# Depthwise taps of one layer spread over three engines: two of DVE's five made by ACT and added by Pool

## The reference, cut to what matters

```python
def _L2_conv_ref(x, w_dw, w_pw):
    C = x.shape[1]
    u_dw, s_dw = _quant_per_channel_dw(w_dw)
    y = lax.conv_general_dilated(x, _ste(w_dw, u_dw), window_strides=(1, 1), padding=((1, 1), (1, 1)),
                                 dimension_numbers=DN, feature_group_count=C)
    y = y / s_dw
    u_pw, s_pw = _quant_global(w_pw)
    y = lax.conv_general_dilated(y, _ste(w_pw, u_pw), window_strides=(1, 1), padding=((0, 0), (0, 0)),
                                 dimension_numbers=DN)
    return y / s_pw
...
x = x + _L2_conv_ref(_gn(x), L2_conv_w_dw, L2_conv_w_pw)
```

## Time and profile before

| | us |
|---|---|
| median of 3 runs | 474.39 |
| lowest, highest | 474.2, 477.4 |
| the profiled execution | 480.05 |
| its span, first to last instruction | 478.3 |
| PE busy in the span | 399.5 |
| DVE busy | 336.7 |
| ACT busy | 246.6 |
| POOL busy | 195.4 |

### The profile page before, as it was taken

The page is one execution under the profiler, slowest core; times in us unless marked ns, Lnnn a source line. Parts: engine busy times, 40 slices in busy tenths (PEclk is TensorE's granted clock), DMA queues, the critical chain, the costliest instruction groups (busy, mean ns, idle before and its releaser), DMA issues.

```text
span 478.3 us, 14126 instructions
## 1 busy us (share of the span) xinstructions
PE 399.5 (84%) x4971; PEld 290.6 (61%) x4971; DVE 336.7 (70%) x786; ACT 246.6 (52%) x554; POOL 195.4 (41%) x326
## 2 busy tenths in 40 slices
PE   0257889999998978899999999999979895758673
PEld 0257578888887856678787787877753221334341
DVE  0588388777877727767777677777827997576782
ACT  0010567877787354566566655666343321465772
POOL 8011166667566714443434344443531534012212
PEclk9999999999999889999999999999998999576985
DMA  8700000000000000000000000000000000000101
GB/s 283 137 5 0 1 3 3 1 0 0 0 0 0 1 2 1 1 3 1 0 0 0 0 0 0 0 0 0 2 3 0 0 0 1 0 16 17 30 21 49
DMA packets 8510, 7.01 MB, mean 15 GB/s; under 512 B 5058, under 2 KB 8130, under 8 KB 8354
## 3 DMA queue, kind: packets, MB, share of 16 engines
q1 hardware_dynamic: 3984, 5.26, 3.6%
q10 hardware_dynamic: 4498, 1.38, 1.7%
HBM read 5.06 MB, written 1.57 MB: 14 GB/s over the span
## 4 chain that ended last, share of the span: by engine, by line
PE 68%; DVE 13%; issue 7%; ACT 6%; DMA 3%; POOL 1%; DVEq 1%; ACTq 1%; POOLq 0%
PE bank L752 11%; PE bank L779 11%; PE bank L720 11%; PE bank L761 9%; PE bank L730 6%; PE bank L1294 5%; PE bank L822 4%; DVE conv L1213 3%; PE bank L809 3%; DMA table<-in_L_conv_rpb_table 3%; PE bank L1222 2%; PE bank L561 2%; PE bank L824 1%; DVE stats L590 1%; ACT kvT L1329 1%
## 5 line engine op out<-in xcount | busy, mean ns | idle before, releaser
L978 POOL TENSOR_TENSOR probs<-probs,row_max 128x384 f32<-128x384 f32 x128 | 105.2, 828 | 125.5 <-DVE row_max L942 124.4
L938 DVE TENSOR_TENSOR probs<-bank,bias 128x384 f32<-128x384 f32 x128 | 65.4, 553 | 58.3 <-PE bank L752 58.0
L843 ACT ACTIVATE probsT<-bank 128x384 f32<-128x384 f32 x128 | 60.9, 492 | 66.7 <-PE bank L761 66.7
L942 DVE TENSOR_REDUCE row_max<-probs 128x6 f32<-128x384 f32 x128 | 68.2, 545 | 0.9
L761 PE MATMUL bank<-cst,probs 128*128 128x128 f32 x384 | 63.0, 282 | 0.0
L752 PE MATMUL bank<-k,q 64*64 64x128 f32 x1536 | 58.4, 284 | 3.9 <-ACT k L888 2.2
L779 PE MATMUL bank<-v,probsT 128*64 128x18 f32 (+1 forms) x1536 | 57.9, 220 | 1.7 <-ACT probsT L843 0.9
L779 PEld LDWEIGHTS bank<-v,probsT 128*64 128x64 f32 x1536 | 50.3, 138 | 13.3 <-issue 11.2
L752 PEld LDWEIGHTS bank<-k,q 64*64 64x64 f32 x1536 | 42.7, 136 | 24.6 <-issue 24.5
L904 DVE COPY v<-bank 64x384 f32<-64x384 f32 (+1 forms) x96 | 46.7, 487 | 11.9 <-PE bank L730 9.7
L761 PEld LDWEIGHTS bank<-cst,probs 128*128 128x128 f32 x384 | 44.7, 142 | 10.3 <-issue 4.4
(11 more groups left out here) (143 smaller groups left out, 622.3 us busy)
## 6 DMA issues: line engine op xcount, KB each, us to landing
rel_bc<-in_L_conv_rel_index SPq DMA_DIRECT2D x1, 2048.0 KB, 9.3
x<-in_x SPq DMA_DIRECT2D x4, 384.0 KB, 12.3
out_dram<-y_out SPq DMA_DIRECT2D x8, 192.0 KB, 2.1
w<-in_L_conv_w_qkv ACTq DMA_DIRECT2D x1, 432.0 KB, 5.0
cst<-in_consts ACTq DMA_DIRECT2D x1, 421.0 KB
p<-in_L_conv_w_out ACTq DMA_DIRECT2D x1, 144.0 KB, 4.9
pos<-in_L_conv_pos_emb SPq DMA_DIRECT2D x8, 2.0 KB
b_qk<-in_L_conv_qkv_b ACTq DMA_DIRECT2D x8, 0.1 KB, 6.9
```

What stands on the lines that cost most here:

```text
L843: nc.scalar.activation(probsT[w][:, :], ps_probsT[w % 2][:, 0:NP * 128], ACT.Exp).then_inc(L.s.probsT_sb, 1)
L938: nc.vector.tensor_tensor(out, scores, b, ALU.add).then_inc(L.s.biased, 1)
L942: nc.vector.tensor_reduce(row_max[w][:, :], probs[w][:, :, :], AX.X, ALU.max).then_inc(L.s.maxed, 1)
L978: nc.gpsimd.tensor_tensor(probs[w][:, :, :], probs[w][:, :, :], by_row(row_max[w]), ALU.subtract).then_inc(L.s.shifted, 1)
```

## The change

ACT makes taps 0 and 1, as two activations that scale by the channel's weight: tap 0 goes into `conv[par]`, tap 1 into a second buffer (a third of `relu3[par]`, which layer 3 uses later). Pool adds the second buffer to `conv[par]` (the join). DVE waits for the join and adds taps 2 to 4, three scalar_tensor_tensor instead of one tensor_scalar and four. PE's four taps and the pointwise stay. ACT's two activations come behind the padding of the same pair; Pool's join of pair j+2 comes behind the residual of pair j, and the joins of pairs 0 and 1 come behind layer 1's residuals.

```diff
-        DVE_TAPS = 9 - PE_TAPS
+        SUM_TAPS = 9 - PE_TAPS
+        DVE_TAPS = SUM_TAPS - 2
+        second = [t[:, 0, :].rearrange("c (y x) -> c y x", x=SIDE) for t in relu3]
+
+        def act_first_tap(act, j, par):
+
+            act.wait_ge(l2_norm, j * 2 + 2)
+            wait(act, l2_pw, j - 1)
+            nc.scalar.activation(conv[par][:, :, :], tap_of(par, 0), ACT.Copy, scale=dw_u[:, 0:1]).then_inc(l2_first, 1)
+            wait(act, l2_joined, j - 1)
+            nc.scalar.activation(second[par], tap_of(par, 1), ACT.Copy, scale=dw_u[:, 1:2]).then_inc(l2_first, 1)
+
+        def pool_join(pool, j, par):
+
+            pool.wait_ge(l2_first, j * 2 + 2)
+            nc.gpsimd.tensor_tensor(conv[par][:, :, :], conv[par][:, :, :], second[par], ALU.add).then_inc(l2_joined, 1)
 
         def dve_depthwise(dve, j, par):
 
-            dve.wait_ge(l2_norm, j * 2 + 2)
-            wait(dve, l2_pw, j - 1)
+            dve.wait_ge(l2_joined, j + 1)
             y = conv[par][:, :, :]
-            for t in range(DVE_TAPS):
-                if t == 0:
-                    ins = nc.vector.tensor_scalar(y, tap_of(par, t), dw_u[:, 0:1], None, ALU.mult)
-                else:
-                    dve.wait_ge(l2_tap, j * DVE_TAPS + t)
-                    ins = nc.vector.scalar_tensor_tensor(y, tap_of(par, t), dw_u[:, t:t + 1], y, ALU.mult, ALU.add)
-                ins.then_inc(l2_tap, 1)
+            for i in range(DVE_TAPS):
+                if i:
+                    dve.wait_ge(l2_tap, j * DVE_TAPS + i)
+                nc.vector.scalar_tensor_tensor(y, tap_of(par, 2 + i), dw_u[:, 2 + i:3 + i], y,
+                                               ALU.mult, ALU.add).then_inc(l2_tap, 1)
...
             act_l2_out(act, j, par)
             if nxt2:
                 act_pad(act, j + 2, par)
+                act_first_tap(act, j + 2, par)
...
             pool_l2_residual(pool, j, par)
+            if nxt2:
+                pool_join(pool, j + 2, par)
...
-            act_pad(act, 0, 0)
-            act_pad(act, 1, 1)
+            for j in range(2):
+                act_pad(act, j, j)
+                act_first_tap(act, j, j)
...
             for s in (B - 2, B - 1):
                 pool_residual(pool, L1, s)
+            for j in range(2):
+                pool_join(pool, j, j)
             pair_loop(pool, pool_l2, norm_2, norm_3)
```

More of the change, by code:

```diff
@@ L1183, in x_pair @@
             return x[:, bass.ds(j * N2, N2)]
-        l2_norm, l2_tap, l2_pw, l2_y, l2_res = (sem("l2_" + n) for n in ("norm", "tap", "pw", "y", "res"))
+        l2_norm, l2_first, l2_joined, l2_tap, l2_pw, l2_y, l2_res = (sem("l2_" + n) for n in
+                                                                     ("norm", "first", "joined", "tap", "pw", "y", "res"))
         def act_pad(act, j, par):
@@ L1221, in pe_pointwise @@
             for t in range(PE_TAPS):
-                nc.tensor.matmul(o, tapT[:, t, :], tap_of(par, DVE_TAPS + t), start=(t == 0), stop=False)
+                nc.tensor.matmul(o, tapT[:, t, :], tap_of(par, SUM_TAPS + t), start=(t == 0), stop=False)
             pe.wait_ge(l2_tap, j * DVE_TAPS + DVE_TAPS)
```

## The result

The changed kernel took 482.12 us (median of 21 runs, 477.02 to 486.01) against 477.14 us for the kernel before (median of 21 runs beside them, 474.20 to 479.52). The ratio is 1.0084, with a 95% interval of 1.0054 to 1.0114: slower by 0.84%, some 4 us. It is taken over the fast runs and leaves out three slow ones of the changed kernel (485.5 to 486.0 us, those with the lowest granted clock); the two medians, over all runs, lie 4.98 us apart. I had forecast 1.4 us less. The more numerous runs put the kernel before at 477.14, not at the 474.39 of its first three, but also as a ratio the forecast (0.997) has the wrong sign.

What follows compares the result with a forecast made beforehand. DVE was taken to bound layer 2, PE close behind. Pointwise shifts of +0.8 at the start, +1.5 at pair 3 and -1.6 at pair 7 led to -1.4 at the end: 474.39 - 1.4 = 473.0 us, range 470.6 to 477.3.

Steps and rivals of the forecast that it cites:

- What bounds the kernel: Layer 2's loop: DVE is the bound, 5.08 us per pair, with PE close behind at 4.29.
- the 0.79 us per pair that PE allows at most: Layer 2: however much DVE is relieved, PE's 4.29 us of the 5.08 period caps the gain per pair.
- the closed chain: Layer 2: padding, two ACT taps, join and DVE taps take 9.05 us per two pairs, 4.53 per pair.
- Costs of the parts: Layer 2: an ACT tap 0.69 us, a Pool join 1.27 to 1.72, DVE's taps near 1.0 on the mean.
- DVE and Pool holding each other up: Layer 2: a Pool add delays DVE's next tap by 0.89 us and waits up to 0.46 itself.
- The norm: End of layer 2: Pool's group norm for layer 3 still ends 5.7 us after DVE's taps of pair 6.
- The start: First pairs of layer 2: pointwise of pairs 0 and 1 +0.8 us, of pair 2 -0.5.
- my -1.4: End of layer 2: the last residual ends 1.4 us earlier, layer 3 unchanged, so the whole time falls by 1.4.
- Pair 3: Layer 2: the join queues behind Pool's norm and residual; PE idles about 3.1 us, the pointwise comes 1.5 later.
- Pairs 4 to 7 PE-bound at full clock: End of layer 2: pair 4 PE-bound at 4.29 us, pair 5 chain-bound; shifts +0.7, +0.4, -0.4, -1.6.
- rival C: Layer 2, pair 3's idle: PE's clock falls, slowing pair 4 by 1.7 to 4.29 us; total +0.3 to +2.9; chance 0.25.
- The range: Whole kernel: 470.6 to 477.3 us, counted from a median of 474.39.

Runs made afterwards that it cites:

- the control: The changed kernel with layer 2's hardware loop (pairs 2 to 5) written out, nothing else different; ratio to the kernel before 1.0063.
- before_gap3: The kernel before, layer 2's loop written out, with four useless DVE taps (3.0 us) ahead of pair 3's last tap; ratio to before 1.0045.
- u_fill03: The control plus useless matmuls, two before pair 0's pointwise and three before pair 3's; ratio to the kernel before 1.0005.
- the fills: The control with three useless matmuls before pair 3's pointwise (ratio to before 1.0022), and with two more before pair 0's (1.0005).
- u_after: The changed kernel with layer 2's hardware loop written out, the control for the other runs; ratio to the kernel before 1.0063.
- u_pair3_dve: The control with pair 3 alone made as before the change, all five taps by DVE; ratio to the kernel before 1.0066.
- u_start_fill3: The control with pairs 0 and 1 made as before the change and three useless matmuls in pair 3's gap; ratio to the kernel before 1.0015.
- u_start_dve: The control with pairs 0 and 1 made as before the change, all five taps by DVE; ratio to the kernel before 1.0003.

## Why the prediction was wrong

- *What bounds the kernel, and the 0.79 us per pair that PE allows at most:* right. Pairs 4 to 5 took 4.29. Pairs 5 to 6 took 4.55, which looks like the 4.53 forecast for the closed chain, but is not it: PE idled only 0.09 us there, in the control the same step takes 4.38 with no idle, and pair 4 to pair 6 took 8.84 and 8.67 against 9.05. The chain did not govern.
- *Costs of the parts, DVE and Pool holding each other up:* right in size (0.72, 1.27 to 1.70, 0.9 per collision). The norm was not as free as I said: DVE's small add (line 607) took 0.57 beside a join instead of 0.15, and Pool's first step of the norm 0.79 instead of 0.53, so Pool's norm for layer 3 ended 6.4 us after pair 6's taps, where I had carried over the 5.7 of before.
- *The start, +0.8 at pair 0 and -0.5 at pair 2:* the first mis-sized term. I took 364.73 of the earlier trace rows as what DVE's taps set, while it was PE at half clock that set it: DVE had finished these taps at 363.1. My place for the changed kernel's own pointwise, 5.98 after the first tap, was right (5.95 measured); what I compared it with was not. With the clock up, the kernel before has its pointwise of pair 0 3.66 us after the first tap and that of pair 2 14.66 (before_gap3, whose gap comes later). The changed kernel with its gaps filled has them at 5.95 and 15.14. The start costs 2.3 at pair 0 and still 0.5 at pair 2, where I had a gain of 0.5. A kernel before with its clock up would have a stretch of 14.66 + 31.60 (pair 2 to layer 3 in its profile, 406.31 - 374.71) = 46.26; u_fill03 has 46.40, which agrees with its ratio of 1.0005. So my -1.4 was some 1.5 too good, 1.0 of it at the start and the rest about the 0.7 at the norm. And the gap of 2.27 us at pair 0, which can bring the clock down by itself, was in none of my cases.
- *Pair 3:* right in its mechanism and its idle (3.17 against 3.1); the pointwise came 22.81 us after the first tap against 22.13 forecast.
- *Pairs 4 to 7 PE-bound at full clock:* the step that failed. This is rival C, at 0.25: the clock fell behind the gap of pair 3 in the profiles of the change and of its control, and pair 3 to pair 4 took 7.40 and 6.07 us against 4.37 where the gap was filled. That is 3.0 and 1.7, inside the 1.7 to 4.3 that I priced; the lower price took four of eight tap matmuls as slow, a number that no row gave, so its agreement is in part luck. Even C, at +0.3 to +2.9, would have fallen short of the measured 4: I added it to a sum that was 1.5 too good and left out the second fall, behind pair 0, which cost 1.7 to 3.4 where it happened (6.06 to 7.72 in the table, against 4.37). And I gave it a quarter, though I had the idle of 3.1 us beside a row in which the clock fell.
- *The range:* it was counted from 474.39, the median of three runs; 21 runs gave 477.14. Three runs of a kernel whose time moves by 1% with its clock do not set a level to a microsecond.

What stays open: which executions have the clock fall at the start, at pair 3 or at both cannot be read from runs without a profile (they give only the clock's mean), so how the 4 us divide between them on average is known only from the fills (by the ratios 2.0 us for pair 3's and 0.8 more for pair 0's, each with an interval wider than that).

## What to carry to other kernels

Work that is taken off the bound engine and handed to two others in a row lengthens the chain at its first use and after every pause of their queues; count the start and the place behind a long instruction as carefully as the steady state. A wait that PE meets costs its length, and more if the clock falls behind it and PE is the bound there (here 1.7 to 3.4 us more, behind waits of 1.6 to 3.2); where another engine is the bound, the fall can cost nothing. Before a start cost is read from a profile, look whether PE's clock was up there: a slow PE hides what the new chain will cost.

## What the runs showed of the hardware that I had not expected

The clock fell behind gaps of 2.27 us (u_after, pair 0), 2.48 us (u_pair3_dve) and once 1.59 us (u_start_fill3), all shorter than the 3.1 at which I called it uncertain. Over the same 1.58 us in u_start_dve it stayed up. In all the profiles here layer 2 has ten idle stretches of PE of 2.27 us or more, and the clock fell at every one, sometimes up to 0.9 us after PE had begun to work again; at 1.07 us and below it fell at none. (The falls over pair 0's taps, as in the earlier trace rows, come behind the gaps of layer 1.) The Trainium skill's warning of idle gaps ("TensorE: Matmul & The Clock Gate", § Why this matters for your kernels) holds here, at shorter gaps than it names. A few useless matmuls paid: filling the gap ahead of layer 3 took 0.5% off two kernels with no other change. And small DVE adds are not free beside a Pool add: line 611 took 1.19 us beside the join of pair 2, where it has 0.16 alone:

```profile
369.21 1.26 POOL L1217 TENSOR_TENSOR conv<-conv,relu 96x512 f32<-96x512 f32 x1 [0.99 <-ACT relu L1212]
369.31 1.19 DVE L611 TENSOR_TENSOR gn_in<-gn_sum 96x8 f32<-96x8 f32 x1
```
